# Four mixers with expert layers: two expert results of a token summed on TensorE instead of GpSimd

## The reference, cut to what matters

```
x = x + L0_conv(_ln_c(x), ...)          # then t = t + L0_ffn(_ln_t(t), ...)   1 expert per token
x = x + L1_conv(_ln_c(x), ...)          # then t = t + L1_ffn(_ln_t(t), ...)   2 experts per token
x = x + L2_conv(_ln_c(x), ...)          # then t = t + L2_ffn(_ln_t(t), ...)   2 experts per token
x = x + L3_conv(_ln_c(x), ...)          # then t = t + L3_ffn(_ln_t(t), ...)   2 experts per token
```

```
def _ln_c(v, eps=1e-06):
    m = jnp.mean(v, axis=-1, keepdims=True)
    s = jnp.var(v, axis=-1, keepdims=True)
    return (v - m) / jnp.sqrt(s + eps)
```

## Time and profile before

| | us |
|---|---|
| median of 3 runs | 2589.05 (2588.59 to 2589.72) |
| profiled execution, its own time | 2590.67 |
| span of the profiled execution | 2588.9 |
| TensorE busy (matmuls) | 1772.6, 68% |
| VectorE busy | 1695.7, 66% |
| GpSimd busy | 1061.8, 41% |
| ScalarE busy | 1056.6, 41% |

### The profile page before, as it was taken

The page is one execution under the profiler, slowest core; times in us unless marked ns, Lnnn a source line. Parts: engine busy times, 40 slices in busy tenths (PEclk is TensorE's granted clock), DMA queues, the critical chain, the costliest instruction groups (busy, mean ns, idle before and its releaser), DMA issues. The chain is left out here.

```text
span 2588.9 us, 44772 instructions
## 1 busy us (share of the span) xinstructions
PE 1772.6 (68%) x10287; PEld 1291.4 (50%) x10304; DVE 1695.7 (66%) x4992; ACT 1056.6 (41%) x2271; POOL 1061.8 (41%) x993
## 2 busy tenths in 40 slices
PE   1476333399348888389998157629974999929992
PEld 1232233388334433178887124318863544419992
DVE  6998699488757777434443677636648577765664
ACT  2333465277233333145554213304434444416661
POOL 0143133244102334434444307747763055546662
PEclk9788655599669999699999668759996999959996
DMA  2000100121210001121111411113324101113236
GB/s 67 0 1 1 65 24 25 42 64 55 74 66 16 24 28 34 42 64 58 57 59 38 140 35 50 49 54 103 95 90 163 37 32 34 34 54 94 85 89 205
DMA packets 171900, 151.82 MB, mean 59 GB/s; under 512 B 28958, under 2 KB 151590, under 8 KB 171746
## 3 DMA queue, kind: packets, MB, share of 16 engines
q1 hardware_dynamic: 141794, 90.82, 12.1%
q0 software_dynamic: 29952, 59.26, 6.5%
HBM read 83.77 MB, written 68.79 MB: 59 GB/s over the span
## 5 line engine op out<-in xcount | busy, mean ns | idle before, releaser
L1033 POOL DMA_INDIRECT returned<-channel_major x488 | 481.0, 986 | 456.3 <-DVE channel_major L992 325.0
L878 PE MATMUL psum<-channel_major 128*128 128x128 f32 x3360 | 461.3, 278 | 0.9 <-ACT channel_major L925 0.9
L941 ACT ACTIVATE channel_major<-psum,bias_columns 128x128 f32<-128x128 f32 x1104 | 323.2, 367 | 293.6 <-PE psum L878 292.9
L894 PE MATMUL psum<-expert_weights,channel_major 128*128 x2784 | 427.9, 289 | 0.6 <-DVE channel_major L981 0.6
L878 PEld LDWEIGHTS psum<-channel_major 128*128 128x128 f32 x3360 | 421.2, 195 | 1.1 <-issue 1.1
L706 POOL DMA_INDIRECT dispatched<-rows_first_choice,slot x192 | 191.8, 999 | 530.0 <-DVE rows_second_choice L632 366.6
L894 PEld LDWEIGHTS psum<-expert_weights,channel_major 128*128 128x128 f32 x2784 | 349.3, 191 | 25.1 <-issue 1.9
L706 POOL DMA_INDIRECT dispatched<-rows_second_choice,slot x192 | 195.4, 1018 | 67.5 <-issue 65.4
L992 DVE TENSOR_SCALAR channel_major<-psum,channel_major 128x128 f32<-128x128 f32 x416 | 144.9, 348 | 97.7 <-PE psum L894 93.1
L969 DVE COPY channel_major<-expert_weights 128x512 f32 (+1 forms) x272 | 100.0, 368 | 157.6 <-PE psum L878 150.6
L326 PE MATMUL psum<-identity,rows_first_choice 128*128 128x128 f32 x256 | 41.5, 322 | 195.4 <-DVE rows_first_choice L313 182.6
(11 more groups left out here) (338 smaller groups left out, 3456.6 us busy)
## 6 DMA issues: line engine op xcount, KB each, us to landing
channel_major<-dispatched SPq DMA_DIRECT2D x488, 65.0 KB
expert_weights<-returned SPq DMA_DIRECT2D x12, 1024.0 KB, 10.4
rows_second_choice<-returned SPq DMA_DIRECT2D x8, 1024.0 KB, 10.8
returned<-channel_major POOLq DMA_INDIRECT x488
expert_weights<-in_L_ffn_w SPq DMA_DIRECT2D x3, 2048.0 KB, 8.9
residual<-in_x SPq DMA_DIRECT2D x8, 512.0 KB, 7.2
rows_first_choice<-returned SPq DMA_DIRECT2D x4, 1024.0 KB, 8.8
out<-residual SPq DMA_DIRECT2D x8, 512.0 KB, 6.0
```

The costliest lines, as they stand in the source:

```text
L878: ins = pe.matmul(k.ps[:, PSH + u % 2, j * P:(j + 1) * P], wc[:, u % 2, j * P:(j + 1) * P], xt[:, u % 2, :], start=True, stop=True)
L894: ins = pe.matmul(bank, gs[:, u % HB, j * P:(j + 1) * P], second[:, bass.ds(e, 1), j, :].rearrange("p a c -> p (a c)"), start=(b2 is None ...
L941: ins = act.activation(hs[:, u % HB, cols], k.ps[:, PSH + u % 2, cols], f["act"], bias=bcol[:, bass.ds(e * J + j, 1)])
L1033: pool.indirect_dma_start(out=k.returned[0:N * K, :], out_offset=bass.IndirectOffsetOnAxis(ap=rt[:, u, C:C + 1].bitcast(I32), axis=0), in_ ...
```

## The change

The GpSimd part of the block is gone. TensorE gets `add_choices(b)` for each of the 8 images ahead of its transposes: it waits for the load of image b, and from image 2 on also for VectorE's residual addition of image b-2, which frees the two PSUM banks (4 and 5, or 6 and 7). For each half of an image (4 tiles, 512 columns, one bank) it multiplies the first result by the identity, starting the bank, and then the second result by the identity, accumulating. That is 4 matmuls per image. The last one raises the semaphore that GpSimd raised before. VectorE adds the two banks, 1024 columns of PSUM, to the residual in one instruction.

```diff
+    def sums(b):
+        return k.ps[:, 4 + 2 * (b % 2):6 + 2 * (b % 2), :]
...
-        if choices == 2:
-            @block.gpsimd
-            def _(pool):
-                for b in range(B):
-
-                    pool.wait_ge(s_back[b].h, s_back[b].base + 16)
-                    pool.tensor_tensor(back[b][:, :, 0:C], back[b][:, :, 0:C], back[b][:, :, C:2 * C],
-                                       ALU.add).then_inc(s["choices_added"].h, 1)
...
-                if choices:
+                if choices == 2:
+                    xs = k.x[:, tiles, :].rearrange("p t c -> p (t c)")
+                    ch.link(dve.tensor_tensor(xs, xs, sums(b).rearrange("p a n -> p (a n)"), ALU.add))
+                elif choices:
                     ch.link(dve.tensor_tensor(k.x[:, tiles, :], k.x[:, tiles, :], back[b][:, :, 0:C], ALU.add))
...
         @block.tensor
         def _(pe):
+            def add_choices(b):
+                pe.wait_ge(s_back[b].h, s_back[b].base + 16)
+                if b >= 2:
+                    pe.wait_ge(*when("norm_step", (b - 2) * per + 1))
+                for half in range(2):
+                    for c in range(2):
+                        ins = pe.matmul(sums(b)[:, half, :].rearrange("p (t c) -> p t c", c=C), k.ident[:],
+                                        back[b][:, half * 4:half * 4 + 4, c * C:(c + 1) * C], start=(c == 0), stop=(c == 1))
+                ins.then_inc(s["choices_added"].h, 1)
+
+            if choices == 2:
+                for b in range(B):
+                    add_choices(b)
```

## The result

The changed kernel takes 2594.82 us (median of 16 runs, 2590.24 to 2596.46) against 2589.53 for the kernel before in the same comparison (16 runs, 2586.07 to 2591.23): a ratio of 1.0018, interval 1.0011 to 1.0025. That is 5 us slower where 7.5 us faster was forecast, and outside the range. A second comparison on one chip gave 1.0017 (1.0008 to 1.0026). The profiled execution took 2594.90 us, its span 2593.2.

What follows compares the result with a forecast made beforehand. VectorE, slowed by GpSimd's adds, was taken to bound both stretches; savings of 3.75 us in layer 2 and 3.76 in layer 3, together 7.5, bring the median from 2589.05 to 2581.5 us, range 2579 to 2588.

Steps and rivals of the forecast that it cites:

- What bounds the kernel now: Layers 2 and 3, up to the statistics: VectorE bounds, GpSimd's adds costing it about 5.2 us per stretch; otherwise 2.80 per image.
- a block that lasts a whole GpSimd instruction: Shared-port lock between VectorE and GpSimd: would promise up to 16 us per stretch; set aside for the rows' 5.2.
- VectorE's adds from PSUM, 1.22 us: VectorE's 16 residual adds with one operand in PSUM: 1.22 us each, against 1.21, so +0.01 us per image.
- What comes to TensorE, "64 matmuls": TensorE sums in two layers: 64 matmuls, four per image, 0.43 us each at 2.4 GHz, 1.72 us per image.
- Image 0: First image of each stretch: four matmuls at 1.2 GHz take 3.78 us; in layer 2 VectorE starts 1.44 us later.
- The time at which the clock rises, 3 to 6 us: TensorE's clock at the start of each stretch: goes from 1.2 to 2.4 GHz 3 to 6 us after the first matmul.
- Cost 0: Image 1 on TensorE: even with 6 us at the lower clock, summed at 6.57 us, before VectorE asks at 6.62.
- Transfers and banks hidden, transposes still at the lower clock: Both stretches: loads of 2.72 us per image and PSUM bank waits cost nothing; first transposes stay at lower clock, gain 0.
- the rival which keeps TensorE at 1.2 GHz: TensorE at 1.2 GHz all stretch, 3.42 us per image, each stretch 0.6 us later, 2590.2 us total; chance 6%.
- The sign named for the clock: Sign that the forecast is wrong in size through the clock: VectorE waits for psum image after image.
- The fear that the clock would fall back between images: TensorE's clock comes late or falls back at times: 2.5 to 5 us of gain lost, 2584 to 2586.5 us; chance 13%.
- The sum: Statistics end 3.75 us earlier in layer 2, 3.76 in layer 3, together 7.5 us; median 2581.5 us.

Runs made afterwards that it cites:

- e2: Kernel before without GpSimd's additions; VectorE adds only the first result, the second is left out: 2573.28 us against 2588.93, ratio 0.9939.
- e1: Changed kernel with half the matmuls, only the first of a token's two results going through TensorE: 2579.82 us against the kernel before's 2588.93, ratio 0.9968.
- e3: Changed kernel plus 12 identity matmuls ahead on TensorE to bring the clock up: 2588.27 us against the kernel before's 2588.93, ratio 1.0000.
- e10: Changed kernel, unedited, measured again beside the kernel before on one chip: 2594.27 us against 2590.47, ratio 1.0017.
- e7: Against the kernel before: GpSimd sums images 0, 2, 4, 6, TensorE the others, 30 matmuls ahead on TensorE: 2781.05 us against 2789.25, ratio 0.9976.
- e5: Against the kernel before: GpSimd sums images 0, 3, 6, TensorE the other five behind 12 extra matmuls: 2584.46 us against 2588.93, ratio 0.9985.
- e8: Against the kernel before: GpSimd sums images 0, 2, 4, 6, TensorE the others, no matmuls ahead: 2788.75 us against 2789.25, ratio 0.9992.
- e9: Unedited copy of e6 measured again beside the kernel before on another chip: 2580.85 us against 2590.47, ratio 0.9959.
- e6: Kernel before, but ScalarE copies each GpSimd sum to PSUM and VectorE adds it from there: 2777.24 us against 2789.25, ratio 0.9962.

## Why the prediction was wrong, step by step

- *What bounds the kernel now*: right. VectorE, slowed by GpSimd's additions, 5.2 us per stretch; without them the steps are 2.80 us and the stretch 22.56 us (e2; 22.55 forecast). Only the reason for setting aside a block that lasts a whole GpSimd instruction was wrong: it took every VectorE add to meet a whole GpSimd add, 16 us for a stretch. An add of VectorE meets what is left of a running one, 0.6 us for most, and the rows fit such a block in all 12 cases (under e2). It changed nothing in the sum.
- *VectorE's adds from PSUM, 1.22 us*: right, 1.220 to 1.222 us.
- *What comes to TensorE, "64 matmuls"*: the step that failed. Each float32 matmul of the program is two matmul instructions on the engine, each with its own weight load, so 128 came (and e1, with half of them, has 64). The price of 0.43 us (0.85 at the lower clock) was right for one instruction, and I multiplied it by the program's count. An image costs 3.43 us, not 1.72, which is more than VectorE's 2.80: the sign turned on this. It could be read before: the line L1946 is executed 128 times in the program (8 images x 16 steps) and has x256 in the page, and L1763, which the program executes twice per image, is the x4 of the earlier trace rows.
- *Image 0*: 3.78 us became 5.48 and 6.81, for the same reason and with the clock as foreseen: four of eight instructions at 1.2 GHz in layer 2 and the fifth in part, and all eight begun at 1.2 GHz in layer 3. e3 shows its share: 1.7 and 3.1 us.
- *The time at which the clock rises, 3 to 6 us*: right (3.6 and 6.2 us, and 2.9 and 4.0 in e10), but "Cost 0" assumed slack that a bound engine doesn't have.
- *Transfers and banks hidden, transposes still at the lower clock*: right (386 GB/s; 8 + 8 transposes in 3.68 us at 1463.74).
- *Rivals*: the pace of 3.43 us per image is that of the rival which keeps TensorE at 1.2 GHz (3.42), and it came with the clock at 1.00: its arithmetic fits, its mechanism is not what happened. Even so it forecast 0.6 us per stretch, since it had image 0 at 3.78. The sign named for the clock, VectorE waiting for psum image after image, appeared too, and pointed at the wrong cause. The fear that the clock would fall back between images had no object here, since TensorE never paused; e7, where it does pause, shows 1.00 through pauses of 1.6 to 1.8 us, and in e5 the clock did fall back.
- *The sum*, with the measured pieces in place of the forecast ones: 5.48 + 7 x 3.43 + 2.93 = 32.45 us in layer 2, and with 6.81 for image 0 it is 33.78 in layer 3, together +6.0 us against before; the medians moved by +5.3. With half the instructions (e1) the stretches are 7.2 us shorter than before, and 7.5 was the forecast: its method was sound for the load that it had counted.

## What to carry to other kernels

Before an operation is priced by a row, set the row's count against the number of times that the program executes the line: if the row has twice as many, the price of one in the row is half the price of the operation. Moving work from a side engine to an idle one pays only while its price per item stays below the step of the engine that sets the end, here 2.80 us, and here the idle engine's first item was the dear one. When two engines disturb each other, moving an operand can be enough: the GpSimd additions could stay, once VectorE no longer read both operands from the same memory.

## What the runs showed of the hardware that I had not expected

- GpSimd and VectorE disturb each other only in some pairs. Beside a GpSimd add of 128x1024, a VectorE add with both operands in on-chip memory takes 1.69 to 3.35 us instead of 1.21 and GpSimd's up to 3.33 instead of 2.35; all 14 VectorE adds that were lengthened (12 before, 2 in e8) end 1.08 to 1.09 us after the GpSimd add beside which they began; with one operand in PSUM both keep their times (1.20 to 1.22 and 2.33 to 2.35, e9). The Trainium skill, page "Advanced Engine Details and Errata", section "GPSIMD Details", says that the two share a read and a write interface and conflict for VectorE instructions with two inputs in on-chip memory; the traces agree.
- A float32 matmul of 128x512 is two instructions (32 give 64 in e1, 64 give 128 in the changed kernel), together 0.86 us per matmul at 2.4 GHz and 1.71 at 1.2 GHz.
- In e5 the granted clock fell back behind a pause of 2.58 us (0.50 from 1432 to 1433), in e7 behind pauses of 1.6 to 1.8 us it did not (1.00). The two differ also in what came ahead of the pause: work at the lower clock alone in e5, work at the full clock in e7. So these runs don't show that the length of the pause decides. With TensorE continuously busy the clock rose after 3.6, 6.2, 2.9 and 4.0 us in four stretches of the same program (the changed kernel and e10), as worked out from its mean over windows of 1 us.
- Why the second chip takes 2789 us for the kernel before stays open. Its stretches are not the reason: they are 25.97 and 26.00 us in e6 there, and 25.97 and 25.96 in the same kernel on another chip (e9).
